# First experts of a four-layer model kernel: weights held and rows moving, third pieces of two blocks in the two halves of the array, no transposes between the products, weights loaded per block

## The chip, the core and the metric

The kernel runs on one core of a Trainium2 chip. The metric is the device time of one execution in microseconds (us). Times of single instructions are in nanoseconds (ns) where the view gives them so.

## The reference, cut to what matters

The model has four layers on x of shape (8, 512, 256), all in f32: linear attention, a mixture of 8 experts (two for each token) with a shared expert, windowed attention, and a mixture of 8 experts (one for each token). The change lies in the second layer:

```python
hg = jnp.einsum('th,ehi->eti', xf, wg)        # xf: 4096 tokens x 256; wg, wu: 8 x 256 x 352
hu = jnp.einsum('th,ehi->eti', xf, wu)
eo = jnp.einsum('eti,eih->eth', jax.nn.silu(hg) * hu, wd)     # wd: 8 x 352 x 256
y = jnp.einsum('te,eth->th', wdense, eo)      # wdense: two weights a token, else 0
shared = jax.nn.silu(xf @ swg) * (xf @ swu) @ swd
return (y + shared).reshape(B, S, H)
```

## The kernel before, in words

A stage that is called mix here does the first attention, the shared expert and the routing. Routing sorts the 8192 (token, expert) pairs into 71 blocks (`NBLK0`) of 128 rows, each block with one expert, whose number is in `blk_expert`. Then `pe_experts0` and its counterparts on the other engines run the first experts, block by block. Then come the windowed attention and the second experts.

For block b of the first experts:

- GpSimd (POOL) gathers the 128 rows from `normed` in HBM into one of three buffers `xs0` (L1839, `pool_rows`).
- TensorE (PE) transposes them, two transposes of 128x128 (L715, `pe_turn_rows`); ScalarE (ACT) copies the result to `xsT0` (L1076).
- PE computes the up products (L757). The transposed rows are the operand that is held in the array, 128x128, and the expert's weights move past it, 352 columns at a time: `wg` into one PSUM bank, `wu` into another. The weights of all eight experts, 5.8 MB, lie in SBUF as `wu0`; four loads of 1408 KB put them there at the kernel's start (L2027).
- ACT takes the silu of the first bank into `hsil` (L1085), VectorE (DVE) multiplies by the second (L1647). The result has tokens on the partitions.
- PE transposes it in three pieces of 128, 128 and 96 (L745), DVE copies them to `aT0` (L1641, L1642).
- PE computes the down product (L736): `aT0` held in three pieces, `wd0` moving, 256 columns. DVE copies it to `y0` (L1634), and SyncE (SP) stores it to `results` (L2044).

Each f32 matmul of the program is two instructions in the trace, each with its own load of the held operand (LDWEIGHTS, engine PEld), so L757 has 8 a block, L736 6; a transpose is one.

No scheduler is involved: each engine's order is that of the Python loops. In step s of `pe_experts0`, PE does the down product of block s-5, the transposes of the product of block s-4, the up products of block s-3 and the transposes of the rows of block s-2. A wait on a semaphore stops everything behind it on that engine. The waits in the PE code are the bank's last reader (`fill`), and the semaphore of the operand. SP's own queue in this stage holds the 71 stores of results and nothing else; SP issues a DMA in the order of its program, and waits at a wait. The register that picks an expert's weights (`value_load` of `blk_expert`) is read on PE, twice a block.

Of the kernel before, what the change touches and what calls it, by code (L numbers as in the profile page):

```python
# [44 lines left out]
DC = 3  # L45
IC = [P, P, INTER - 2 * P]
SC = [P] * 5 + [SI - 5 * P]
NC = len(SC)
# [139 lines left out]
def build(nc, a, out):  # L188
    ctx = ExitStack()
    with ctx:  # L190
# [3 lines left out]
        def sem(name):  # L194
            return ctx.enter_context(nc.semaphore(name))
# [66 lines left out]
        wu0 = carve(arena, 0, NX, EC, 2 * INTER)  # L262
        wd0 = carve(arena, 11264, NX, DC, E)
# [62 lines left out]
        y0 = carve(work, 5376, 3, E)  # L326
        hsil = carve(work, 6144, 2, INTER)
        aT0 = carve(work, 6848, 2, DC * P)

# [16 lines left out]
        x_loaded = [sem(f"x_loaded{b}") for b in range(B)]  # L346
        wa_loaded, bias_loaded, wu0_loaded, wd0_loaded, sh_loaded, wc_loaded = (
            sem(n) for n in ("wa_loaded", "bias_loaded", "wu0_loaded", "wd0_loaded", "sh_loaded", "wc_loaded"))
        w1_got, w2_got = ([sem(f"{n}_got{i}") for i in range(2)] for n in ("w1", "w2"))
# [16 lines left out]
        xsT_made, y_made = ([sem(f"{n}_l{l}") for l in range(2)] for n in ("xsT_made", "y_made"))  # L366
        sil0_made, hsil_made, aT0_made, h_made, tokens_made, part_made = (
            sem(n) for n in ("sil0_made", "hsil_made", "aT0_made", "h_made", "tokens_made", "part_made"))
        (picked, counted, so_far_made, placed, pick_step, scored, experts_listed, list_set, one_hot_made,
# [20 lines left out]
        def emptied(kind, *k):  # L390
# [34 lines left out]
            if kind == "up0":  # L425
                b, u = k
                return (sil0_made, hsil_made)[u], b + 1
            if kind == "h0":
                return aT0_made, k[0] + 1
            if kind == "down0":  # L430
# [289 lines left out]
        def pe_experts0(e):  # L720
            o_ring = (6, 7)
            e.wait_ge(route_step, EXPERT_AT)
            e.wait_ge(wu0_loaded, 16 * 4)
            e.wait_ge(wd0_loaded, 16 * 3)
            for s in range(NBLK0 + 5):
                b = s - 5
                if b == NBLK0 - 1:

                    pe_shared_up(e, BM, 0, FIRST_RING, range(1))
                if b >= 0:  # L730
                    bk = next_of(o_ring)
                    fill(e, ("down0", b), bk)
                    e.wait_ge(aT0_made, b + 1)
                    x = e.value_load(blk_expert[0:1, 0, b:b + 1], min_val=0, max_val=NX - 1)
                    for c in range(DC):
                        m = e.matmul(psum[:, bk, 0:E], aT0[0:IC[c], b % 2, c * P:(c + 1) * P],  # L736
                                     wd0[0:IC[c], bass.ds(x, 1), c, :], start=(c == 0), stop=(c == DC - 1))
                    m.then_inc(bank_full[bk], 1)
                b = s - 4
                if 0 <= b < NBLK0:  # L740
                    bk = next_of(T_RING)
                    fill(e, ("h0", b), bk)
                    e.wait_ge(hsil_made, b + 1)
                    for c in range(DC):
                        m = e.transpose(psum[0:IC[c], bk, c * P:(c + 1) * P], hsil[:, b % 2, c * P:c * P + IC[c]],  # L745
                                        ident[:, :])
                    m.then_inc(bank_full[bk], 1)
                b = s - 3
                if 0 <= b < NBLK0:
                    pair = ((2, 3), (0, 1))[b % 2]  # L750
                    e.wait_ge(xsT_made[0], b + 1)
                    for u in range(2):
                        fill(e, ("up0", b, u), pair[u])
                    x = e.value_load(blk_expert[0:1, 0, b:b + 1], min_val=0, max_val=NX - 1)
                    for u in range(2):
                        for c in range(EC):
                            m = e.matmul(psum[:, pair[u], 0:INTER], xsT0[:, b % 2, c * P:(c + 1) * P],  # L757
                                         wu0[:, bass.ds(x, 1), c, u * INTER:(u + 1) * INTER],
                                         start=(c == 0), stop=(c == EC - 1))
                        m.then_inc(bank_full[pair[u]], 1)  # L760
                b = s - 2
                if 0 < b < NBLK0:
                    pe_turn_rows(e, 0, b, xs0, next_of(T_RING))

# [307 lines left out]
        def act_turned_rows(e, l, b, xsT):  # L1072
            if b >= 2:
                e.wait_ge(*done["up0" if l == 0 else "up1", b - 2, 1])
            e.wait_ge(*done["rows", l, b])
            e.activation(xsT[:, b % 2, :], psum[:, bank_of["rows", l, b], 0:E], ACT.Copy).then_inc(xsT_made[l], 1)  # L1076

        def act_experts0(e):
            for s in range(NBLK0 + 5):
                b = s - 3  # L1080
                if 0 <= b < NBLK0:
                    if b >= 2:
                        e.wait_ge(*done["h0", b - 2])
                    e.wait_ge(*done["up0", b, 0])
                    e.activation(hsil[:, b % 2, :], psum[:, bank_of["up0", b, 0], 0:INTER],  # L1085
                                 ACT.Silu).then_inc(sil0_made, 1)
                b = s - 2
                if 0 <= b < NBLK0:
                    act_turned_rows(e, 0, b, xsT0)

        def act_attention(e):
# [535 lines left out]
        def dve_experts0(e):  # L1627
            for s in range(NBLK0 + 5):
                b = s - 5
# [5 lines left out]
                b = s - 4  # L1635
                if 0 <= b < NBLK0:
                    bk = bank_of["h0", b]
                    if b >= 2:
                        e.wait_ge(*done["down0", b - 2])
                    e.wait_ge(*done["h0", b])  # L1640
                    e.tensor_copy(aT0[:, b % 2, 0:2 * P], psum[:, bk, 0:2 * P])  # L1641
                    e.tensor_copy(aT0[0:IC[2], b % 2, 2 * P:3 * P], psum[0:IC[2], bk, 2 * P:3 * P]).then_inc(aT0_made, 1)  # L1642
                b = s - 3
                if 0 <= b < NBLK0:
                    e.wait_ge(sil0_made, b + 1)
                    e.wait_ge(*done["up0", b, 1])
                    e.tensor_tensor(hsil[:, b % 2, :], hsil[:, b % 2, :], psum[:, bank_of["up0", b, 1], 0:INTER],  # L1647
                                    ALU.mult).then_inc(hsil_made, 1)

# [356 lines left out]
        def sp_second_weights(e, k):  # L2006
            if k < 2:
                e.wait_ge(*done["again", (NU - 4, NU - 2)[k], TPB - 1, G - 1])
            else:
# [3 lines left out]
                        a["w2"][bass.ds(x, 1), :, :].rearrange("x p n -> p (x n)")).then_inc(w2_got[k % 2], 16)  # L2013

        def sp_mix(e):
            for b in range(B):
# [7 lines left out]
            e.dma_start(sdn[0:SC[5], 5, :], a["swd"][5 * P:SI, :]).then_inc(sh_loaded, 16)  # L2024
            for i, n in enumerate(("wg", "wu")):
                for c in range(EC):
                    e.dma_start(wu0[:, :, c, i * INTER:(i + 1) * INTER],  # L2027
                                a[n][:, c * P:(c + 1) * P, :].rearrange("x p n -> p x n")).then_inc(wu0_loaded, 16)
            for c in range(DC):
# [10 lines left out]
        def _(e):  # L2040
            sp_mix(e)
            for b in range(NBLK0):
                e.wait_ge(y_made[0], b + 1)
                e.dma_start(results[b * P:(b + 1) * P, :], y0[:, b % 3, :]).then_inc(result_kept[b % 3], 16)  # L2044
# [51 lines left out]
```

## Time and profile before

| what | value |
|---|---|
| three runs | 1450.71, 1465.5, 1467.46 us; median 1465.5 |
| profiled execution, span | 1452.0 us |
| first experts in it | about 308 to 617 us |
| PE busy, share of the span | 1394.5 us, 96% |
| DVE, ACT, POOL busy | 699.3, 467.8, 446.9 us |
| DMA over the span | 204.29 MB, mean 141 GB/s |

The profile also cuts the span in 40 slices of 36.3 us. In those of the first experts PE is 9 tenths busy or more, the DMA engines 1 to 2 tenths, at 50 to 70 GB/s. In the second experts, from about 1145 us on, which load their weights for each block, the DMA engines are 9 tenths busy at 320 to 350 GB/s. The granted clock of TensorE is 1.0 of full speed (2.4 GHz) in most slices.

Busy time counts from a matmul's start to its modelled end, and successive matmuls overlap; so what a matmul costs in a row of them is the distance between two starts, not its mean duration. In a merged row of the timeline, with n instructions in a time t and one of them taking d, that distance is (t - d)/(n - 1).

### The profile page before, as it was taken

The page shows a single profiled execution, that of the slowest core. Times are in us where ns is not written, and L with a number is a line of the kernel's source. Part 1 is how long each engine was busy: PE and PEld are TensorE (multiplying, and loading weights), DVE is VectorE, ACT ScalarE, POOL GpSimd, SP SyncE. Part 2 cuts the span into 40 slices and gives each one's busy share as a digit, 9 for nine tenths or more (in the row PEclk, how much of TensorE's full clock was granted, in tenths as well). Part 3 has the DMA queues.
Part 4 walks back from the last instruction along what each step waited for, and adds up shares of the span by engine and source line. Part 5 has one row for each costly group of instructions (what it writes and reads, how often), then busy time and mean ns, then how long its engine had stood idle before and what let it go on. Part 6 is the DMA issues. An engine that isn't in the chain of part 4 may idle for free.

```text
span 1452.0 us, 23966 instructions
## 1 busy us (share of the span) xinstructions
PE 1394.5 (96%) x7789; PEld 1034.4 (71%) x7789; DVE 699.3 (48%) x2502; ACT 467.8 (32%) x915; POOL 446.9 (31%) x533
## 2 busy tenths in 40 slices
PE   6899999999999999999999999999998999999998
PEld 4666655667777777755666667666666789999998
DVE  5743345723333333334878878788778213210000
ACT  1211111012111111121576665666656512111111
POOL 1100000035222222161444544544423434344442
PEclk9889999999999999999999999999999999999999
DMA  9400100011121211114544635545432578899996
GB/s 333 140 15 30 58 1 0 1 37 62 60 65 58 66 59 61 50 54 116 166 133 135 186 113 153 161 137 142 140 115 68 191 295 330 330 321 346 337 345 217
DMA packets 88583, 204.29 MB, mean 141 GB/s; under 512 B 11373, under 2 KB 45295, under 8 KB 78480
## 3 DMA queue, kind: packets, MB, share of 16 engines
q1 hardware_dynamic: 72512, 167.99, 35.4%
q0 software_dynamic: 12096, 32.13, 7.3%
q10 hardware_dynamic: 3856, 2.64, 0.6%
q8 instruction: 67, 1.10, 0.3%
q14 instruction: 52, 0.43, 0.1%
HBM read 151.48 MB, written 52.17 MB: 140 GB/s over the span
## 4 chain that ended last, share of the span: by engine, by line
PE 86%; DVE 7%; issue 4%; ACT 2%; DMA 0%; DVEq 0%; POOLq 0%; POOL 0%; ACTq 0%
PE psum L757 12%; PE psum L633 10%; PE psum L924 10%; PE psum L934 9%; PE psum L736 6%; PE psum L644 6%; PE psum L830 5%; PE psum L783 5%; PE psum L854 3%; PE psum L805 3%; DVE work L1763 2%; PE psum L884 2%; PE psum L560 2%; PE psum L863 2%; PE psum L715 2%
## 5 line engine op out<-in xcount | busy, mean ns | idle before, releaser
L1763 DVE CUSTOM_DVE_ANT_0 work<-psum,mask 128x384 bf16<-128x384 f32 (+1 forms) x512 | 230.8, 485 | 71.7 <-PE psum L783 69.3
L757 PE MATMUL psum<-arena,work 128*128 x568 | 185.0, 469 | 0.6 <-issue 0.6
L783 PE MATMUL psum<-kz,qT 96*128 96x384 f32 (+1 forms) x512 | 171.0, 401 | 13.5 <-DVE small L1763 12.6
L1839 POOL DMA_INDIRECT work<-normed,token_of x71 | 67.3, 948 | 342.3 <-PE psum L715 206.6
L633 PE MATMUL psum<-arena 128*128 128x512 f32 x320 | 152.3, 621 | 0.0
L924 PEld LDWEIGHTS psum<-arena 128*128 128x128 f32 x1248 | 145.3, 192 | 2.2 <-issue 0.4
L924 PE MATMUL psum<-arena 128*128 128x128 f32 x1248 | 146.1, 275 | 0.0
L1158 ACT ACTIVATE arena<-psum 128x384 f32<-128x384 f32 x256 | 112.2, 494 | 91.7 <-PE psum L805 90.8
L934 PE MATMUL psum<-arena 128*128 128x256 f32 x624 | 141.0, 379 | 0.0
L757 PEld LDWEIGHTS psum<-arena,work 128*128 128x128 f32 x568 | 102.1, 189 | 51.4 <-issue 2.3
L783 PEld LDWEIGHTS psum<-kz,qT 96*128 96x128 f32 x512 | 89.8, 194 | 66.5 <-DVE small L1763 40.3
L1624 DVE TENSOR_TENSOR arena<-psum,arena 128x256 f32<-128x256 f32 x39 | 16.6, 425 | 245.1 <-PE psum L934 245.1
L805 PE MATMUL psum<-qT,kz 100*128 100x384 f32 (+1 forms) x512 | 128.9, 328 | 3.8 <-ACT arena L1158 3.6
L934 PEld LDWEIGHTS psum<-arena 128*128 128x128 f32 x624 | 115.6, 190 | 14.1
L1905 POOL TENSOR_SCALAR_AFFINE_SELECT arena<-arena 128x512 f32<-128x512 f32 x96 | 63.0, 656 | 179.1 <-ACT arena L1158 161.5
L1186 ACT ACTIVATE arena<-psum 128x1024 f32<-128x1024 f32 x39 | 39.9, 1023 | 223.8 <-PE psum L924 223.8
L633 PEld LDWEIGHTS psum<-arena 128*128 128x128 f32 x320 | 62.4, 200 | 67.9 <-issue 66.7
L736 PE MATMUL psum<-arena,work 128*128 (+1 forms) x426 | 104.0, 380 | 0.2 <-issue 0.2
L805 PEld LDWEIGHTS psum<-qT,kz 100*128 100x128 f32 x512 | 89.7, 193 | 14.7 <-ACT arena L1158 12.9
L1647 DVE TENSOR_TENSOR work<-work,psum 128x352 f32<-128x352 f32 x71 | 37.0, 521 | 130.7 <-PE psum L757 130.7
L1160 ACT ACTIVATE arena<-psum 128x512 f32<-128x512 f32 x128 | 75.7, 596 | 57.6 <-PE psum L805 57.1
L644 PE MATMUL psum<-arena,work 128*128 128x256 f32 (+1 forms) x384 | 91.7, 381 | 2.3 <-DVE X L1324 2.3
(226 smaller groups left out, 2070.7 us busy)
## 6 DMA issues: line engine op xcount, KB each, us to landing
arena<-in_w SPq DMA_DIRECT2D x78, 1024.0 KB, 7.1
strips<-hi SPq DMA_DIRECT2D x64, 256.0 KB
kz<-strips SPq DMA_DIRECT2D x64, 192.0 KB, 3.1
qT<-strips SPq DMA_DIRECT2D x32, 384.0 KB, 4.6
results<-work SPq DMA_DIRECT2D x71, 128.0 KB, 1.7
strips<-lo SPq DMA_DIRECT2D x32, 256.0 KB
normed<-work SPq DMA_DIRECT2D x14, 512.0 KB, 3.0
X<-in_x SPq DMA_DIRECT2D x8, 512.0 KB, 9.5
```

The costliest lines, as they stand in the source:

```text
L633: m = e.matmul(psum[0:w, bk, :], sgu[:, k, u, c * P:c * P + w], xnT_all[:, b, k, :], start=(k == 0), stop=(k == EC - 1))
L644: m = e.matmul(psum[:, banks[t // 2], (t % 2) * E:(t % 2 + 1) * E], aT_s[0:w, q, t * P:(t + 1) * P], sdn[0:w, c, :], start=(c == 0 and t % ...
L736: m = e.matmul(psum[:, bk, 0:E], aT0[0:IC[c], b % 2, c * P:(c + 1) * P], wd0[0:IC[c], bass.ds(x, 1), c, :], start=(c == 0), stop=(c == DC ...
L757: m = e.matmul(psum[:, pair[u], 0:INTER], xsT0[:, b % 2, c * P:(c + 1) * P], wu0[:, bass.ds(x, 1), c, u * INTER:(u + 1) * INTER], start=(c ...
L783: m = e.matmul(psum[:, bk, at:at + w], qT[0:ROWS_S, slot, half, i * P:(i + 1) * P], kz[slot][0:ROWS_S, hd, lo_key:hi_key], start=True, sto ...
L805: m = e.matmul(psum[:, bk, at:at + w], kz[slot][0:ROWS_T, hd, j * P:(j + 1) * P], qT[0:ROWS_T, slot, half, lo_q:hi_q], start=True, stop=True)
L830: m = e.matmul(psum[32 * hh:32 * hh + 32, bk, lo:hi], v32[:, b % 2, j, G * g + hh, :], pT(u, j)[:, hh, 0:hi - lo], start=(j == 0), stop=(j ...
L924: m = e.matmul(psum[:, bk, q * P:(q + 1) * P], w1_now[k % 2][:, c, at:at + P], xsT1[:, k % 2, c * P:(c + 1) * P], start=(c == 0), stop=(c ...
L934: m = e.matmul(psum[:, bk, 0:E], hT1[:, k % 2, c * P:(c + 1) * P], w2_now[k % 2][:, c, :], start=(c == 0), stop=(c == HC - 1))
L1158: e.activation(pT(u, j)[:, hd, 0:w], psum[:, bk, 0:w], ACT.Exp, scale=1.0 / E ** 0.5).then_inc(p_exped, 1)
L1160: e.activation(pT(u, j)[:, hd - 1:hd + 1, 0:w], psum[:, bk, :].rearrange("p (h n) -> p h n", h=2), ACT.Exp, scale=1.0 / E ** 0.5).then_inc ...
L1763: e.tensor_tensor_reduce(masked[:, n % 2, 0:w], psum[:, bank_of["scores", u, i, hd], at:at + w], mask[:, P - off:P - off + w], 1.0, MASKED ...
```

## The change

The up products change sides. `pe_up0` holds 128x128 pieces of the weights in the array and moves the 128 transposed rows past them; the product comes out with the intermediate features on the partitions, as the down product needs it. The transposes of L745 and DVE's copies L1641 and L1642 are gone. Features 0 to 255 of `wg` and `wu` are four pieces (two of each), all in one PSUM bank. The last 96 features of each are split in 64 and 32: the 64 of both make one held piece of 128 columns; the 32 of both make one of 64 columns, and those of an even block go to the lower 64 columns of the array, those of the odd block after it to the upper 64. These third pieces are computed for two blocks at a time, in `pe_rest0`, after the odd block's `pe_up0`.

`wu0` now has four buffers of one block's weights each (5632 bytes in each partition, 704 KB). SP loads them per block from `wgu`, an array made on the host before the launch with `wg` and `wu` side by side in the order of use. The down product, the gathers and the transposes of the rows stay; `aT0` has four buffers instead of two. On PE the order within step s is now up (s-3), the third pieces if s-3 is odd, rows (s-2), down (s-5).

```diff
-            e.wait_ge(wu0_loaded, 16 * 4)
             e.wait_ge(wd0_loaded, 16 * 3)
             for s in range(NBLK0 + 5):
+                b = s - 3
+                if 0 <= b < NBLK0:
+                    pe_up0(e, b)
+                    if ends_pair(b):
+                        pe_rest0(e, pair_of(b))
+                b = s - 2
+                if 0 < b < NBLK0:
+                    pe_turn_rows(e, 0, b, xs0, next_of(T_RING))
                 b = s - 5
...
+        def pe_up0(e, b):
+
+            e.wait_ge(xsT_made[0], b + 1)
+            e.wait_ge(wu0_got[b % 4], 16 * (b // 4 + 1))
+            fill(e, ("up0", b), b % 2)
+            for q in range(4):
+                for c in range(EC):
+                    m = e.matmul(psum[:, b % 2, q * P:(q + 1) * P], wu0[:, b % 4, c, q * P:(q + 1) * P],
+                                 xsT0[:, b % 2, c * P:(c + 1) * P], start=(c == 0), stop=(c == EC - 1))
+            m.then_inc(bank_full[b % 2], 1)
+
+        def pe_rest0(e, pair):
+
+            q, bk = pair[0] // 2, 2 + pair[0] // 2 % 2
+            fill(e, ("rest0", q), bk)
+            for b in pair:
+                for c in range(EC):
+                    m = e.matmul(psum[:, bk, b % 2 * P:(b % 2 + 1) * P], wu0[:, b % 4, c, 4 * P:5 * P],
+                                 xsT0[:, b % 2, c * P:(c + 1) * P], start=(c == 0), stop=(c == EC - 1))
+            for c in range(EC):
+                for b in pair:
+                    half = b % 2 * D0
+                    m = e.matmul(psum[half:half + 2 * TAILS[1], bk, 2 * P:3 * P], wu0[:, b % 4, c, 5 * P:2 * INTER],
+                                 xsT0[:, b % 2, c * P:(c + 1) * P], start=(c == 0), stop=(c == EC - 1),
+                                 skip_group_check=True)
+            m.then_inc(bank_full[bk], 1)
...
             for s in range(NBLK0 + 5):
+                b = s - 3
+                if 0 <= b < NBLK0:
+                    if b >= 4:
+                        e.wait_ge(*done["down0", b - 4])
+                    e.wait_ge(sil0_made, b + 1)
+                    e.tensor_tensor(aT0[:, b % 4, 0:2 * P], sil0[:, b % 2, :],
+                                    psum[:, bank_of["up0", b], 2 * P:4 * P], ALU.mult).then_inc(main_made, 1)
+                    if ends_pair(b):
+                        dve_rest0(e, pair_of(b))
                 b = s - 5
...
+        def sp_up0_weights(e, b):
+
+            if b >= 4:
+                e.wait_ge(*done["rest0", (b - 4) // 2])
+            x = e.value_load(blk_expert[0:1, 0, b:b + 1], min_val=0, max_val=NX - 1)
+            e.dma_start(wu0[:, b % 4, :, :].rearrange("p c n -> p (c n)"),
+                        a["wgu"][bass.ds(x, 1), :, :].rearrange("x p n -> p (x n)")).then_inc(wu0_got[b % 4], 16)
...
             sp_mix(e)
+            e.wait_ge(route_step, EXPERT_AT)
+            for b in range(4):
+                sp_up0_weights(e, b)
             for b in range(NBLK0):
+                if 4 <= b + 3 < NBLK0:
+                    sp_up0_weights(e, b + 3)
                 e.wait_ge(y_made[0], b + 1)
                 e.dma_start(results[b * P:(b + 1) * P, :], y0[:, b % 3, :]).then_inc(result_kept[b % 3], 16)
```

On ACT the silu of a block is now 256 columns, and after an odd block three more follow (`act_rest0`: one of 64x256, two of 32x128), ahead of the copy of the next rows to `xsT0`. On DVE `dve_rest0` is one product of 64x256 and two of 32x128.

PE's rows in the first experts, in the middle of the stage. Before, one step (L715 rows of a block, L734 the register and L736 the down product, L745 the transposes of the product, L757 the up products):

```order
L715 MATMUL psum<-ident,work 128x128 [waits rows_got1,xsT_made_l0]
L715 MATMUL psum<-ident,work 128x128
L734 TENSOR_LOAD blk_expert [waits aT0_made,y_made_l0]
L734 ISA x2
...
L736 MATMUL psum<-arena,work 128x256
L745 MATMUL psum<-ident,work 128x128 [waits hsil_made,aT0_made]
L745 MATMUL psum<-ident,work 128x128
L745 MATMUL psum<-ident,work 96x128
L754 TENSOR_LOAD blk_expert [waits hsil_made,sil0_made,xsT_made_l0]
```

Now, the step of an odd block and the head of the next (L763 the four pieces, L773 the 64-feature pieces of two blocks, L778 the 32-feature pieces, L718 the rows, L746 the down product):

```order
L763 MATMUL psum<-work,arena 128x128 [waits main_made,wu0_got3,xsT_made_l0]
L763 MATMUL psum<-work,arena 128x128 x7
L773 MATMUL psum<-work,arena 128x128 [waits aT0_made]
L773 MATMUL psum<-work,arena 128x128 x3
L778 MATMUL psum<-work,arena 64x128 x4
L718 MATMUL psum<-ident,work 128x128 [waits rows_got0,xsT_made_l0]
L718 MATMUL psum<-ident,work 128x128
...
L746 MATMUL psum<-arena,work 128x256
L763 MATMUL psum<-work,arena 128x128 [waits main_made,wu0_got0,xsT_made_l0]
L763 MATMUL psum<-work,arena 128x128 x7
```

The up products moved ahead of the down product of their step, and their first matmul waits for a weight load's semaphore `wu0_got`.

SP's rows. Before, around and in this stage (the loads at the kernel's start are L2027, the stores L2044):

```order
L2027 DMA arena<-in_wg 128x8x352 x2
L2027 DMA arena<-in_wu 128x8x352 x2
...
L2036 DMA arena<-in_wqkvT 128x2x768 [waits bank_full6,bank_full7]
L2037 DMA arena<-in_wpT 128x2x256
L2044 DMA results<-work 128x256 [waits y_made_l0] x71
```

Now, in the middle of the stage (L2091 the store, L2057 and L2058 the load of weights):

```order
L2091 DMA results<-work 128x256 [waits y_made_l0]
L2057 TENSOR_LOAD blk_expert [waits bank_full3]
L2057 ISA x2
L2058 ISA
L2058 DMA arena<-in_wgu 128x1408
L2091 DMA results<-work 128x256 [waits y_made_l0]
```

The load of block b+3's weights stands behind the store of block b-1's result, and so behind the wait for it.

DVE's rows now, two steps in the middle of the stage (L1666 the product of the four pieces, L1681 and L1685 those of the third pieces, L1675 the copy of the down product):

```order
L1666 TENSOR_TENSOR work<-work,psum 128x256 [waits sil0_made,bank_full7]
L1681 TENSOR_TENSOR work<-work,psum 64x2x128 [waits rest_sil]
L1685 TENSOR_TENSOR work<-work,psum 32x128 x2
L1675 COPY work<-psum 128x256 [waits bank_full7,result_kept0]
L1666 TENSOR_TENSOR work<-work,psum 128x256 [waits sil0_made,bank_full6]
L1675 COPY work<-psum 128x256 [waits bank_full6,result_kept1]
```

In the step of an odd block the copy of a down product now stands behind the three products of the third pieces.

## Rows read from the trace of the kernel before

**Rows 1.** Windows: busy us (count) by engine, granted clock, DMA share, GB/s.

```profile
308.00:617.00 309.00, 307.74 (x1352) 222.41 (x1351) 105.63 (x285) 59.70 (x141) 80.25 (x79) 1.00 0.19 60
```

**Rows 2.** Timeline, middle of the stage: start, us, engine, line, count [idle before].

```profile
441.46 0.49 PE L745 MATMUL psum<-ident,work 128*128 128x128 f32 x3
441.73 0.42 DVE L1634 COPY work<-psum 128x256 f32<-128x256 f32 x1 [0.99 <-PE psum L736]
...
441.80 2.59 PE L757 MATMUL psum<-arena,work 128*128 x8
...
442.19 0.32 SPq L2044 DMA_DIRECT2D results<-work  x1
...
444.22 0.38 PE L715 MATMUL psum<-ident,work 128*128 128x128 f32 x2
...
444.44 1.46 PE L736 MATMUL psum<-arena,work 128*128 x6
...
445.74 0.49 PE L745 MATMUL psum<-ident,work 128*128 128x128 f32 x3
```

**Rows 3.** Timeline and group, second experts: 128 columns moving past 128 held.

```profile
1254.33 3.73 PE L924 MATMUL psum<-arena 128*128 128x128 f32 x32
...
L924 PE MATMUL psum<-arena 128*128 128x128 f32 x1248 | 146.1, 275 | 0.0
```

**Rows 4.** Timeline and group: 32 held columns; 128 held columns at 512 moving.

```profile
1140.12 2.36 PE L830 MATMUL psum<-arena 128*32 128x256 f32 x32
...
617.33 4.88 PE L633 MATMUL psum<-arena 128*128 128x512 f32 x11
...
L633 PE MATMUL psum<-arena 128*128 128x512 f32 x320 | 152.3, 621 | 0.0
```

**Rows 5.** Timeline, mix: from 128 held columns to 64.

```profile
118.86 2.02 PE L575 MATMUL psum<-arena,work 128*128 128x128 f32 x16
...
120.81 1.07 PE L581 MATMUL psum<-work,arena 128*64 128x512 f32 x2
```

**Rows 6.** Groups: ACT and DVE forms nearest the new ones; busy, mean ns.

```profile
L1076 ACT ACTIVATE work<-psum 128x256 f32<-128x256 f32 x71 | 27.2, 383 | 67.6 <-PE psum L715 67.6
L1642 DVE COPY work<-psum 96x128 f32<-96x128 f32 x71 | 19.7, 277 | 0.0
```

**Rows 7.** Lines L2002 and L2003 on SP: ns min/median/max, first and last start.

```profile
L2002 SPq TENSOR_LOAD <-blk_expert x39: 263/273/623, 1122.2 to 1426.3; - x39
L2003 SPq DMA_DIRECT2D arena<-in_w x39: 337/338/387, 1123.1 to 1427.1; - x39
```

**Rows 8.** DMA issues: KB each, us from issue to landing; 1123:1129, then the stage.

```profile
arena<-in_w SPq DMA_DIRECT2D x1, 1024.0 KB, 4.9
...
results<-work SPq DMA_DIRECT2D x70, 128.0 KB, 1.7
```

**Rows 9.** Timeline: four of PE's six idle times over 1.2 us at full clock.

```profile
47.73 2.02 PE L575 MATMUL psum<-arena,work 128*128 128x128 f32 x16 [2.10 <-DVE work L1234]
...
249.50 1.75 PE L644 MATMUL psum<-arena,work 128*128 128x256 f32 x7 [2.31 <-DVE X L1324]
...
689.63 0.92 PE L783 MATMUL psum<-kz,qT 96*128 96x384 f32 x2 [1.38 <-DVE small L1763]
...
1130.42 0.82 PE L805 MATMUL psum<-qT,kz 100*128 100x384 f32 x2 [1.29 <-ACT arena L1158]
```

**Rows 10.** Windows as rows 1, of the stretches behind these four.

```profile
49.70:56.50 6.80, 5.37 (x31) 3.54 (x31) 5.98 (x21) 1.19 (x2) 2.66 (x2) 1.00 0.25 83
249.50:256.30 6.80, 6.80 (x28) 4.51 (x29) 3.12 (x7) 0.60 (x1) 0.00 (x0) 1.00 0.01 2
692.20:699.00 6.80, 5.86 (x22) 4.85 (x21) 4.39 (x23) 1.57 (x3) 1.12 (x2) 0.50 0.45 138
1132.50:1139.30 6.80, 6.80 (x30) 6.44 (x29) 2.09 (x9) 1.64 (x4) 1.20 (x2) 0.50 0.00 0
```

**Rows 11.** Timeline: 512-column matmuls at half the clock.

```profile
150.92 5.91 PE L633 MATMUL psum<-arena 128*128 128x512 f32 x7
```

More of the change, by code:

```diff
@@ L46 @@
 IC = [P, P, INTER - 2 * P]
+TAILS = (D0, INTER - 2 * P - D0)
 SC = [P] * 5 + [SI - 5 * P]
@@ L259, in carve @@
             return v
-        wu0 = carve(arena, 0, NX, EC, 2 * INTER)
+        wu0 = carve(arena, 0, 4, EC, 2 * INTER)
         wd0 = carve(arena, 11264, NX, DC, E)
@@ L326, in build @@
         y0 = carve(work, 5376, 3, E)
-        hsil = carve(work, 6144, 2, INTER)
-        aT0 = carve(work, 6848, 2, DC * P)
+        sil_thin = carve(work, 4864, P)
+        sil_wide = carve(work, 4992, 2, P)
+        sil0 = carve(work, 6144, 2, 2 * P)
+        aT0 = carve(work, 6656, 4, DC * P)
         masked = carve(work, 4096, 2 * 3 * P // 2).bitcast(BF16).rearrange("p (s n) -> p s n", s=2)
@@ L346, in build @@
         x_loaded = [sem(f"x_loaded{b}") for b in range(B)]
-        wa_loaded, bias_loaded, wu0_loaded, wd0_loaded, sh_loaded, wc_loaded = (
-            sem(n) for n in ("wa_loaded", "bias_loaded", "wu0_loaded", "wd0_loaded", "sh_loaded", "wc_loaded"))
+        wa_loaded, bias_loaded, wd0_loaded, sh_loaded, wc_loaded = (
+            sem(n) for n in ("wa_loaded", "bias_loaded", "wd0_loaded", "sh_loaded", "wc_loaded"))
+        wu0_got = [sem(f"wu0_got{i}") for i in range(4)]
         w1_got, w2_got = ([sem(f"{n}_got{i}") for i in range(2)] for n in ("w1", "w2"))
@@ L366, in build @@
         xsT_made, y_made = ([sem(f"{n}_l{l}") for l in range(2)] for n in ("xsT_made", "y_made"))
-        sil0_made, hsil_made, aT0_made, h_made, tokens_made, part_made = (
-            sem(n) for n in ("sil0_made", "hsil_made", "aT0_made", "h_made", "tokens_made", "part_made"))
+        sil0_made, main_made, rest_sil, aT0_made, h_made, tokens_made, part_made = (
+            sem(n) for n in ("sil0_made", "main_made", "rest_sil", "aT0_made", "h_made", "tokens_made", "part_made"))
         (picked, counted, so_far_made, placed, pick_step, scored, experts_listed, list_set, one_hot_made,
@@ L425, in emptied @@
             if kind == "up0":
[L426 to L429, printed above, removed]
+                return main_made, k[0] + 1
+            if kind == "rest0":
+                return aT0_made, min(2 * k[0] + 2, NBLK0)
             if kind == "down0":
@@ L735, in pe_experts0 @@
                     for c in range(DC):
-                        m = e.matmul(psum[:, bk, 0:E], aT0[0:IC[c], b % 2, c * P:(c + 1) * P],
+                        m = e.matmul(psum[:, bk, 0:E], aT0[0:IC[c], b % 4, c * P:(c + 1) * P],
                                      wd0[0:IC[c], bass.ds(x, 1), c, :], start=(c == 0), stop=(c == DC - 1))
                     m.then_inc(bank_full[bk], 1)
[L739 to L760, printed above, removed]
@@ L761, in pe_experts0, with pair_of, ends_pair @@
-                b = s - 2
-                if 0 < b < NBLK0:
-                    pe_turn_rows(e, 0, b, xs0, next_of(T_RING))
+        def pair_of(b):
+            return range(b - b % 2, b + 1)
+        def ends_pair(b):
+            return b % 2 == 1 or b == NBLK0 - 1
+        def pe_up0(e, b):
[7 more added lines that the diff above has]
+            m.then_inc(bank_full[b % 2], 1)
@@ L1073, in act_turned_rows @@
             if b >= 2:
-                e.wait_ge(*done["up0" if l == 0 else "up1", b - 2, 1])
+                e.wait_ge(*done["rest0", (b - 2) // 2] if l == 0 else done["up1", b - 2, 1])
             e.wait_ge(*done["rows", l, b])
@@ L1082, in act_experts0 @@
                     if b >= 2:
-                        e.wait_ge(*done["h0", b - 2])
-                    e.wait_ge(*done["up0", b, 0])
-                    e.activation(hsil[:, b % 2, :], psum[:, bank_of["up0", b, 0], 0:INTER],
+                        e.wait_ge(main_made, b - 1)
+                    e.wait_ge(*done["up0", b])
+                    e.activation(sil0[:, b % 2, :], psum[:, bank_of["up0", b], 0:2 * P],
                                  ACT.Silu).then_inc(sil0_made, 1)
+                    if ends_pair(b):
+                        act_rest0(e, pair_of(b))
                 b = s - 2
@@ L1089, in act_experts0, with act_rest0 @@
                     act_turned_rows(e, 0, b, xsT0)
+        def act_rest0(e, pair):
+            q, n, w = pair[0] // 2, len(pair), TAILS[1]
+            if q >= 1:
+                e.wait_ge(aT0_made, 2 * q)
+            e.wait_ge(*done["rest0", q])
+            bk = bank_of["rest0", q]
+            e.activation(sil_wide[0:D0, 0:n, :], psum[D0:2 * D0, bk, 0:n * P].rearrange("p (b n) -> p b n", b=n), ACT.Silu)
+            for b in pair:
+                half = b % 2 * D0
+                m = e.activation(sil_thin[half:half + w, :], psum[half + w:half + 2 * w, bk, 2 * P:3 * P], ACT.Silu)
+            m.then_inc(rest_sil, 1)
         def act_attention(e):
@@ L1628, in dve_experts0 @@
             for s in range(NBLK0 + 5):
+                b = s - 3
[5 more added lines that the diff above has]
+                                    psum[:, bank_of["up0", b], 2 * P:4 * P], ALU.mult).then_inc(main_made, 1)
+                    if ends_pair(b):
+                        dve_rest0(e, pair_of(b))
                 b = s - 5
@@ L1634, in dve_experts0, with dve_rest0 @@
                     e.tensor_copy(y0[:, b % 3, :], psum[:, bank_of["down0", b], 0:E]).then_inc(y_made[0], 1)
[L1635 to L1648, printed above, removed]
+        def dve_rest0(e, pair):
+            q, n, w = pair[0] // 2, len(pair), TAILS[1]
+            bk, s0 = bank_of["rest0", q], pair[0] % 4
+            e.wait_ge(rest_sil, q + 1)
+            e.tensor_tensor(aT0[0:D0, s0:s0 + n, 2 * P:3 * P], sil_wide[0:D0, 0:n, :],
+                            psum[0:D0, bk, 0:n * P].rearrange("p (b n) -> p b n", b=n), ALU.mult)
+            for b in pair:
+                half = b % 2 * D0
+                e.tensor_tensor(aT0[D0:D0 + w, b % 4, 2 * P:3 * P], sil_thin[half:half + w, :],
+                                psum[half:half + w, bk, 2 * P:3 * P], ALU.mult).then_inc(aT0_made, 1)
         def dve_attention(e):
@@ L2024, in sp_mix @@
             e.dma_start(sdn[0:SC[5], 5, :], a["swd"][5 * P:SI, :]).then_inc(sh_loaded, 16)
[L2025 to L2028, printed above, removed]
             for c in range(DC):
@@ L2080 @@
         "gate0T": g["L0_ffn_gate_w"].T,
-        "wg": g["L0_ffn_wg"], "wu": g["L0_ffn_wu"], "wd": g["L0_ffn_wd"],
+        "wgu": np.concatenate([g[n][:, :, i:j] for i, j, names in (
+            (0, 2 * P, ("L0_ffn_wg", "L0_ffn_wu")), (2 * P, 2 * P + D0, ("L0_ffn_wu", "L0_ffn_wg")),
+            (2 * P + D0, INTER, ("L0_ffn_wu", "L0_ffn_wg"))) for n in names], axis=2)
+               .reshape(NX, EC, P, 2 * INTER).transpose(0, 2, 1, 3).reshape(NX, P, EC * 2 * INTER),
+        "wd": g["L0_ffn_wd"],
         "swg": g["L0_ffn_swg"], "swu": g["L0_ffn_swu"], "swd": g["L0_ffn_swd"],
```

## The prediction

> **What bounds the kernel now.** I read the page first: PE is busy 96% of the span. So the question is whether the stage that changes is paced by PE. The windows view of that stage says yes: PE is busy 307.7 of 309 us, the granted clock is 1.00, DVE is busy a third of the time, and the DMA engines 0.19 of it [rows 1]. Then I read one step in the timeline. L745 starts at 441.46 and again at 445.74, so a block takes 4.28 us. It splits, by the distances between starts, into 0.34 us of L745, 2.42 of L757, 0.22 of L715 and 1.30 of L736 (six instructions, 0.217 each) [rows 2]. No row of PE in it shows idle time: the stage is PE's sum, 71 times. Nothing else is worth time here as long as it hides; and whatever makes PE wait costs in full.
>
> **PE's work after the change.** What L757 did is now done by matmuls that move only 128 columns. The nearest row is L924, the same form: 32 of them in 3.73 us, one lasting 0.275, so (3.73 - 0.275)/31 = 0.111 us each [rows 3]. The weight load of each hides at that pace. For a pair of blocks:
>
> - the four pieces: 2 x 16 instructions x 0.111 = 3.55 us;
> - the 64-feature pieces: 8 x 0.111 = 0.89;
> - the 32-feature pieces: 8 instructions in two halves of the array. L830 holds 32 columns, four heads side by side; 32 of its instructions, half of 256 and half of 384 moving columns, take 2.36 us. At the pace of L633, (4.88 - 0.62)/10 = 0.43 us for 512 columns, they would take 8.5 us one by one, so four do run together [rows 4]. I take two together here: 4 x 0.111 = 0.45; one by one it is 0.89;
> - going to the half-width form and back: the first L581 starts 0.21 us after the last L575 (118.86 + 2.02 - 0.275 = 120.60), against 0.11 inside a row [rows 3, 5]. Above these 0.10 I take 0.15 for each change, since the weight load of the other form doesn't hide either: 0.30 a pair;
> - rows and down product stay: 2 x 0.22 + 2 x 1.30 = 3.04.
>
> The sum is 8.23 us a pair, against 8.56 now: 0.3 us less, 11 us over 35.5 pairs. If the halves don't overlap it is 5 us more than now instead. The removed DVE copies and the second register read on PE are worth nothing, since they lie beside PE's work. The 5.6 MB of loads at the start that fall away are worth nothing either: nothing in the stage before waits for them.
>
> **The added wait.** An odd step's PE work is 1.78 + 0.89 + 0.45 + 0.30 + 0.22 + 1.30 = 4.94 us, an even step's 1.78 + 0.22 + 1.30 = 3.30. The weights of block b+3 are asked for by SP after it has stored the result of block b-1, although their buffer came free a step or two earlier. That result is the last thing of step b+4; the weights are wanted by the first matmul of step b+6. One step lies between. For an odd block b+3 that step is an even one, 3.30 us. Against it stands this chain, from the end of the down product:
>
> - DVE starts 0.11 us later (L736 ends at 445.90, a block earlier at 441.62; L1634 starts at 441.73) and takes 0.42; SP issues the store 0.04 later, in 0.32 [rows 2];
> - in an odd step DVE first has the third pieces. After their last matmul ACT needs 0.1 + 0.38 + 2 x 0.28, DVE 0.06 + 0.42 + 2 x 0.28, by the nearest forms [rows 2, 6]: 2.1 us, while the down product is done 1.8 us after that matmul: 0.3 more;
> - SP then reads the register and issues the load: from the start of TENSOR_LOAD to the DMA, 0.8 us by first and last starts [rows 7];
> - the landing. 1024 KB alone take 4.9 us from the issue, 128 KB 1.7 [rows 8]; on the line between them 704 KB take 3.8. A gather and a store of 128 KB use the same engines in each step, for which I add 0.2: 4.0. The ends are 3.6 (no slower than the line, somewhat faster issue) and 4.9 (as the 1024 KB);
> - 0.1 to PE.
>
> Together 0.11 + 0.3 + 0.42 + 0.04 + 0.32 + 0.8 + 4.0 + 0.1 = 6.1 us. The next step could have started 0.16 before the down product's end (0.38 less 0.22). So PE stands idle 6.1 + 0.16 - 3.30 = 3.0 us before each odd block from about the fifth on: 33 times, 99 us. The ends of the landing make it 2.6 to 3.9, 86 to 129 us. Even blocks don't wait: between their chain's ends lie an odd step and that idle time, 7.9 us. Behind the waiting matmul stands everything of the step: third pieces, rows, down product; ACT, DVE, the gathers and the next load wait with it, so nothing catches up.
>
> **The clock.** An idle time of 3 us is longer than any that PE had at the full clock in this kernel after its start. Of six over 1.2 us I show four: 2.10 and 2.31 us went by and the clock stayed; 1.38 and 1.29, in stretches with other short gaps, were followed within 4 us by 6.8 us at 0.50, which is 1.2 instead of 2.4 GHz [rows 9, 10]. Of the two not shown one was followed by a fall. At 0.50 a matmul takes twice as long: seven L633 in 5.91 us, (5.91 - 0.62)/6 = 0.88 against 0.43 [rows 4, 11]. Each fall thus costs 3.4 us of work if it does not lie over another wait. I take a fall after 7 in 10 of the 33 waits, more than the half seen because these waits are longer: 23 x 3.4 = 78 us. The ends are 16 falls (54 us) and 33 (112 us).
>
> The Trainium skill (TensorE: Matmul & The Clock Gate, HAM oscillation) tells of a kernel that waits some microseconds for a DMA between bursts of matmuls and starts every burst at the lower clock. It speaks against this change. By it all 33 waits are followed by a fall, and the sum below would be 34 us higher; the 2.10 and 2.31 us of these rows, shorter than its waits, had none.
>
> **The sum**, against the profiled execution's own span: 1452.0 - 11 + 99 + 78 = 1618 us. That execution lies 13.5 us below the median of the three runs and 1.3 above the fastest, and I don't know which the runs of the changed kernel will be like; I add half, 7: 1625 us.
>
> **The rivals.**
>
> - *The weights arrive in time.* Four buffers and loads issued three blocks ahead look like enough. Then only PE's work counts: 1452 - 11 + 7 = 1448 us, 1% faster. For it speaks that a load needs only 704 KB in 4.2 us, 170 GB/s, and the second experts move over 320. Against it speaks that this is a matter of when the load is issued: the break-even is an idle time of 0.33 us, a chain of 3.5 instead of 6.1 us, and the load would have to land in 1.4 us, less than 128 KB take now [rows 8].
> - *PE waits, but the clock holds.* 1452 - 11 + 99 + 7 = 1547 us. For it speak the two longest idle times of the trace, after which it held [rows 9, 10]; and PE would be busy 8.2 of 11.2 us.
> - *The clock falls after every wait.* PE waits for a landing of 704 KB, works 8.2 us, waits again, and each of the 33 waits is followed by 6.8 us at 0.50: 1452 - 11 + 99 + 112 + 7 = 1659 us. For it speaks that 1.3 us were enough twice. The Trainium skill's page above has this rule.
> - *Everything at its dear end.* The load takes 4.9 us to land and the halves of the array work one after the other: 30 and 16 us on the forecast, 1671 us. For it speaks that gathers and stores share the engines.
>
> **How the numbers follow.** The forecast, that PE waits and the clock falls after most waits, has a chance of 0.50; its own range is 1588 to 1666 (landing and falls at their ends). The clock holds: 0.18. It falls every time: 0.17. The dear end: 0.07. In time: 0.08. The range 1530 to 1670 leaves out the case in time, part of the dear end and the tails of the others, some 0.2 in all. A measurement of this kernel can tell about 2% from no change. All cases but one are slower by more than that: 0.90; in time is within 2% of 1465.5: 0.08; that leaves 0.02 for faster, a clock in step with cheaper third pieces.
>
> **What would show it.** In the stage of the first experts: L763's first matmul of odd blocks idle about 3 us before it, with the DMA arena<-in_wgu as the releaser, and none before even ones; a pair of blocks at 8.2 us of PE work where the clock is 1.00; the load's landing near 4 us; L778's instructions starting two by two; windows at 0.50 for 6 or 7 us, some 23 of them. The stage would be about 475 us long instead of 309. The prediction is wrong if the waits are short or absent, which would mean that SP gets to the load earlier than the chain says, and off in size if the clock's falls are few or many.

## The result

| | median of runs | runs | span of the profiled execution |
|---|---|---|---|
| before | 1459.99 us | 1450.71, 1454.49, 1465.5, 1467.46 | 1452.0 |
| changed | 1596.83 us | 1588.97, 1593.91, 1599.75, 1600.77 | 1592.0 |

The changed kernel takes 1.094 times as long, 95% interval 1.089 to 1.098. The page of its profile, the parts that changed:

```profile
PE 1431.0 (90%) x8712; PEld 1117.1 (70%) x8712; DVE 690.0 (43%) x2467; ACT 491.6 (31%) x1022; POOL 447.9 (28%) x533
...
L763 PE MATMUL psum<-work,arena 128*128 128x128 f32 x1136 | 169.4, 311 | 101.9 <-issue 98.8
...
arena<-in_wgu SPq DMA_DIRECT2D x71, 704.0 KB, 4.4
```

L763, the four pieces, has 101.9 us of idle time of PE before it, 97.9 of them before the 33 odd blocks from block 5 on and the rest before blocks 0, 1, 2 and 4; L757 of before had none to speak of, and its stage was busy throughout [rows 1]. The releaser is given as "issue", that is, the profile doesn't name what was waited for. The windows of the stage, as rows 1 for before:

```profile
301.30:748.00 446.70, 346.34 (x2275) 305.07 (x2276) 94.43 (x248) 83.05 (x248) 80.45 (x79) 0.90 0.46 149
```

The stage of the first experts is 446.7 us long, from its first up product to the end of its last down product; in the kernel before it was 309.2. That is 137.5 us more. The spans of the two profiled executions differ by 140.0 and the medians by 136.8, so nearly all of the loss is here. The mean granted clock of the stage is 0.90 where it was 1.00. The timeline of a pair of blocks, which answers to rows 2:

```profile
446.78 0.38 PE L746 MATMUL psum<-arena,work 96*128 x1
447.00 0.59 DVE L1685 TENSOR_TENSOR work<-work,psum 32x128 f32<-32x128 f32 x2
447.00 2.05 PE L763 MATMUL psum<-work,arena 128*128 128x128 f32 x16
447.63 0.42 DVE L1675 COPY work<-psum 128x256 f32<-128x256 f32 x1
448.08 0.33 SPq L2091 DMA_DIRECT2D results<-work  x1
448.89 0.38 PE L718 MATMUL psum<-ident,work 128*128 128x128 f32 x2
449.11 1.46 PE L746 MATMUL psum<-arena,work 128*128 x6
...
449.49 0.35 SPq L2058 DMA_DIRECT2D arena<-in_wgu  x1
...
451.13 0.33 SPq L2091 DMA_DIRECT2D results<-work  x1
452.22 0.34 SPq L2058 DMA_DIRECT2D arena<-in_wgu  x1
453.56 0.77 PE L763 MATMUL psum<-work,arena 128*128 128x128 f32 x4 [2.98 <-issue]
```

The down product of an odd step ends at 447.16. DVE copies its result only at 447.63, since it had the third pieces to do (L1685 just ahead). SP stores it at 448.08 and issues the load at 449.49. PE has done the even step by 450.57 and stands idle until 453.56, 4.07 us after the issue. Past block 4 the idle time comes before odd blocks only. In the median of the 33 odd blocks it is 2.01 us from the end of that down product to the load's issue, and 4.27 from there to the first matmul. The clock, in windows around that place:

```profile
454.00:457.40 3.40, 3.40 (x19) 3.40 (x18) 0.00 (x0) 0.38 (x1) 0.00 (x0) 0.50 0.41 171
433.50:454.00 20.50, 14.65 (x108) 12.54 (x107) 4.92 (x13) 4.31 (x13) 3.79 (x4) 1.00 0.52 165
```

Right behind the idle time the clock is at 0.50 for 3.4 us, and PE then does 19 matmuls where at the full clock it does 30. The trace's record of the clock has 24 such stretches in the stage, 85.3 us in all: 23 of 3.4 us and one of 6.8. Each begins during the wait before an odd block or at most 1.4 us after it. For 1.7 of the 85.3 us PE stood idle anyway, so they cost (85.3 - 1.7)/2 = 41.8 us of work. The pairs of blocks show the same: from block 11 on the median is 11.37 us for a pair without such a stretch and 13.12 for a pair with one, 1.75 more.

### The profile page after: what moved, and what is told of

It is laid out like the page before. It is cut to its first block, busy times and chain, and to the rows that moved or that the text cites. A ratio compares the mean times of both kernels' runs of the same rounds, so it can differ in the third digit from the quotient of the medians.

```text
span 1592.0 us, 25699 instructions
## 1 busy us (share of the span) xinstructions
PE 1431.0 (90%) x8712; PEld 1117.1 (70%) x8712; DVE 690.0 (43%) x2467; ACT 491.6 (31%) x1022; POOL 447.9 (28%) x533
## 4 chain that ended last, share of the span: by engine, by line
PE 81%; issue 10%; DVE 6%; ACT 2%; POOL 1%; DMA 1%; DVEq 0%; POOLq 0%; ACTq 0%
PE psum L763 10%; PE psum L942 9%; PE psum L952 9%; PE psum L636 8%; PE psum L746 6%; PE psum L647 5%; PE psum L801 5%; PE psum L848 5%; PE psum L823 3%; PE psum L872 3%; PE psum L773 3%; PE psum L902 2%; PE psum L718 2%; PE psum L563 2%; PE psum L881 2%
## 5 line engine op out<-in xcount | busy, mean ns | idle before, releaser
L763 PE MATMUL psum<-work,arena 128*128 128x128 f32 x1136 | 169.4, 311 | 101.9 <-issue 98.8
L763 PEld LDWEIGHTS psum<-work,arena 128*128 128x128 f32 x1136 | 154.7, 218 | 123.6 <-issue 112.1
L636 PE MATMUL psum<-arena 128*128 128x512 f32 x320 | 146.1, 599 | 0.0
L1666 DVE TENSOR_TENSOR work<-work,psum 128x256 f32<-128x256 f32 x71 | 29.9, 421 | 255.3 <-ACT work L1103 253.4
L1103 ACT ACTIVATE work<-psum 128x256 f32<-128x256 f32 x71 | 27.3, 384 | 305.7 <-PE psum L763 305.7
L746 PE MATMUL psum<-arena,work 128*128 (+1 forms) x426 | 103.8, 380 | 0.0
```

The source lines that it names most:

```text
L636: m = e.matmul(psum[0:w, bk, :], sgu[:, k, u, c * P:c * P + w], xnT_all[:, b, k, :], start=(k == 0), stop=(k == EC - 1))
L746: m = e.matmul(psum[:, bk, 0:E], aT0[0:IC[c], b % 4, c * P:(c + 1) * P], wd0[0:IC[c], bass.ds(x, 1), c, :], start=(c == 0), stop=(c == DC ...
L763: m = e.matmul(psum[:, b % 2, q * P:(q + 1) * P], wu0[:, b % 4, c, q * P:(q + 1) * P], xsT0[:, b % 2, c * P:(c + 1) * P], start=(c == 0), ...
```

## Experiments

All are edits of the changed kernel. "Stage" is measured as above, "idle" is PE's idle time before L763 by its row, "falls" are the stretches at 0.50 that begin in the stage and their length in all. In the runs marked * one stretch of 3.4 us lies at the head of the stage, behind 1.5 us of idle time before block 0; it has nothing to do with the loads. Five rows are single executions: the two that load less, the one that loads nothing, and the two with one half of the array. The three that load less or nothing leave wrong weights in the buffers, and are here for their traces.

| kernel | time | stage | idle | falls |
|---|---|---|---|---|
| before | 1460 | 309.2 | - | 0 |
| changed | 1597 | 446.7 | 101.9 | 24, 85.3 us |
| DVE copies the result first * | 1571 | 421.3 | 76.2 | 17, 58.0 |
| half of each load * | 1527 | 376.6 | 63.5 | 5, 17.1 |
| an eighth of each load * | 1486 | 333.5 | 26.7 | 1, 3.4 |
| wait filled with work * | 1560 | 407.2 | 15.1 | 1, 3.4 |
| loads one block earlier * | 1451 | 304.2 | 3.4 | 0, the one at the head begins 0.06 us ahead of it |
| no loads * | 1451 | 302.3 | 3.2 | 1, 3.4 |
| earlier loads, one half of the array, blocks in turn * | 1484 | 317.5 | 3.1 | 1, 3.4 |
| earlier loads, one half of the array, block by block * | 1470 | 317.7 | 3.3 | 1, 3.4 |
| earlier loads, ACT copies the rows first | 1452 | 305.6 | 5.8 | 0 |

**Loads one block earlier.**

```diff
-                if 4 <= b + 3 < NBLK0:
-                    sp_up0_weights(e, b + 3)
+                if b + 4 < NBLK0:
+                    sp_up0_weights(e, b + 4)
```

> The only edit: SP issues the load of block b+4's weights where it issued that of block b+3, so each load has one more step of PE work to hide behind (8.2 us between the store it stands behind and the use, against a chain of 6.1). Theory (the loss is the place of the load in SP's order, and the clock's falls follow from the wait): no wait of PE for arena<-in_wgu, no fall of the clock in the stage, a stage of about 310 us (PE work 8.2 us a pair, and 0.3 us a pair in which PE waits for ACT's copy of the rows), and a time within 1% of the kernel before, 1450 to 1470 us. Rival (the loads themselves cost: 51 MB share the DMA engines with gathers and stores, or the held-weights form is slower on PE than L924 says): the time stays over 1500 us.

Measured: 1451.2 us, 0.996 times the kernel before (0.992 to 0.9995), with all of the change's matmuls, loads and silus in it.

```profile
440.30 1.46 PE L746 MATMUL psum<-arena,work 128*128 x6
441.61 1.95 PE L763 MATMUL psum<-work,arena 128*128 128x128 f32 x16
443.39 1.06 PE L773 MATMUL psum<-work,arena 128*128 128x128 f32 x8
444.38 0.66 PE L778 MATMUL psum<-work,arena 128*64 128x128 f32 x8
444.96 0.44 PE L718 MATMUL psum<-ident,work 128*128 128x128 f32 x2
445.24 1.46 PE L746 MATMUL psum<-arena,work 128*128 x6
446.54 2.05 PE L763 MATMUL psum<-work,arena 128*128 128x128 f32 x16
448.43 0.38 PE L718 MATMUL psum<-ident,work 128*128 128x128 f32 x2
448.65 1.46 PE L746 MATMUL psum<-arena,work 128*128 x6
449.95 0.27 PE L763 MATMUL psum<-work,arena 128*128 128x128 f32 x1
```

This is its timeline of PE: a pair of blocks from 441.61 to 449.95, 8.34 us without idle time. No odd block waits. One fall lies at the head of the stage, where none was expected. Everything lost was lost by the place of the load in SP's order; traffic and form of the product cost nothing against the kernel before. The theory stands, and its rival falls.

**No loads.** The load in SP's loop is taken out and the wait for it, from block 4 on.

> Loads only the weights of the first four blocks and none after them, and PE doesn't wait for more, so most blocks use the wrong experts' weights. It shows what PE's own order costs with no load and no wait. Theory: a stage of 305 to 312 us at a clock of 1.00, as in the run with the loads one block earlier, and the same time as that one within its noise. Rival (the loads' traffic slows gathers or stores even when nobody waits for the weights): this one is faster than that one by 10 us or more.

Measured: 1450.7 us, stage 302.3 against 304.2, a little under the expected 305. The traffic of 48 MB of weights, once nobody waits for it, costs at most 2 us.

**The wait filled with work.**

```diff
+            fill(e, ("up0", b), b % 2)
+            if b % 2 == 1 and b >= 5:
+                for _ in range(3):
+                    e.matmul(psum[:, b % 2, :], ident[:, :], wd0[:, 0, 0:2, :].rearrange("p c n -> p (c n)"),
+                             start=True, stop=True)
             e.wait_ge(wu0_got[b % 4], 16 * (b // 4 + 1))
-            fill(e, ("up0", b), b % 2)
```

> The changed kernel with work added: before the up products of each odd block from 5 on PE does three f32 matmuls of 512 columns (2.6 us at the full clock) into the bank that the up products then overwrite, ahead of the wait for the weights. It separates the wait's own length from the clock. Theory (each fall of the clock to 0.50 after a wait costs half its length, 34 falls of 3.4 us in the stage, 58 us): falls in the stage go to nearly none, and the time goes down by 45 to 60 us, to about 1540 us, although there is more work. Rival (the falls cost nothing, since the chain through SP sets the pace and PE's slower work hides in it): the time stays within 10 us of the changed kernel's, or goes up.

Measured: 1560.2 us, 37 us less than the changed kernel with 198 matmul instructions more; 1.072 times the kernel before (1.067 to 1.078). PE's timeline and the stage's window:

```profile
440.33 2.74 PE L762 MATMUL psum<-arena,ident 128*128 128x512 f32 x6
443.56 2.05 PE L767 MATMUL psum<-work,arena 128*128 128x128 f32 x16 [0.49 <-DMA arena<-in_wgu]
...
303.00:710.20 407.20, 393.74 (x2473) 305.25 (x2474) 94.43 (x248) 82.99 (x248) 80.26 (x79) 1.00 0.51 164
```

With 0.5 us of this wait left (0.24 in the median), the profile names what ended it, the load. The clock's mean is 1.00, and the stage is 39.5 us shorter. The 41.8 us of the 24 falls, less the one at the head of this stage, would be 40.1. So the falls cost what half their length says, on top of the wait; they don't hide in the chain. The rival falls. The time went down by less than the expected 45 to 60 us, since that expectation took 34 falls where there are 24.

**Less to load.** From block 4 on only the first 704, or 176, of a partition's 1408 numbers are brought.

> The changed kernel, but from block 4 on each load brings only the first half of a block's weights (352 KB), the other half being stale, so those blocks' results are wrong. SP's order is unchanged. Theory (PE's wait is the chain through SP less one even step): the landing goes from 4.4 to about 2.9 us and the idle time before odd blocks from 2.9 to about 1.4 us, 33 x 1.5 = 50 us less; the falls become fewer, so 1480 to 1545 us. Rival (the wait is set by something of fixed length, such as the register read or DVE's order, and not by the landing): the idle time stays over 2.5 us.

> As the run with half a load, but from block 4 on each load brings an eighth of a block's weights (88 KB), so those blocks' results are wrong. With the landing near that of a store of 128 KB, about 1.8 us instead of 4.4, the theory gives an idle time of 2.9 - 2.6 = 0.3 us before odd blocks, no fall of the clock in the stage, and a stage of 304 + 33 x 0.3 = 314 us; the time about 1465 us. It is also the fixed part of the rule that the first rival needed: even a tiny load only just arrives. Rival (a fixed length other than the landing): the idle time stays over 1 us.

Measured: landings of 4.4, 3.0 and 2.0 us (704, 352 and 88 KB), idle times before odd blocks with a median of 2.9, 1.7 and 0.6 us, stages of 447, 377 and 334 us. The half is within its expected range (1527 us), with 0.3 us more idle time than expected. The eighth has 0.6 us of idle time where I expected 0.3; 0.2 of that is its landing, which I took at 1.8 us and which was 2.0. It is 20 us dearer than expected with a stage 20 us longer. The idle time of its 33 odd blocks is 13 us more than the 10 expected. Another 5 us are 0.16 lost at each wait, which I had left out: where PE waits, the last matmul before it runs to its end, and without a wait the next one starts 0.16 us earlier. Its stage has no fall behind a wait for a load, and that of the half has four. The idle time follows the landing nearly one to one (2.4 us less landing, 2.3 us less idle time). Even 88 KB come too late: of the chain of over 6 us, 2.0 are in front of the load.

**DVE's order.** In `dve_experts0` the copy of the down product's result goes ahead of `dve_rest0`.

> The changed kernel, with DVE's copy of the down product's result ahead of its three products of the third pieces; SP's order is that of the change. Theory (the load hangs on that copy through SP): the copy starts 0.1 us after the down product's end instead of 0.47, every load of an odd block is issued 0.36 us earlier, the idle time before odd blocks goes from 2.87 to about 2.5 us, 33 x 0.36 = 12 us less, and a few falls of the clock fewer: 1575 to 1585 us. Rival (the idle time is set by when the load's buffer comes free or by the DMA engines): it stays at 2.9 us.

Measured: 1570.9 us, 1.075 times the kernel before (1.068 to 1.082), 4 us under the expected range. One pair, DVE, SP and PE:

```profile
444.07 1.46 PE L746 MATMUL psum<-arena,work 128*128 x6
...
445.64 0.42 DVE L1673 COPY work<-psum 128x256 f32<-128x256 f32 x1 [2.25 <-PE psum L746]
...
447.26 0.38 PE L718 MATMUL psum<-ident,work 128*128 128x128 f32 x2
...
447.79 1.56 PE L746 MATMUL psum<-arena,work 128*128 x6
...
451.64 3.19 PE L763 MATMUL psum<-work,arena 128*128 128x128 f32 x16 [2.30 <-issue]
```

The copy starts 0.11 us after the down product's end (445.53), as expected. The idle time before odd blocks is 2.2 us in the median, 0.7 less and not 0.36. The rows show where the rest went: the even step's down product now starts 0.53 us after L718 instead of 0.22. By its program it waits for its `aT0`, which the third pieces complete, and then reads a register; in these rows `aT0` comes 1.0 us later behind the odd step's down product than in the pair shown of the changed kernel. So 0.3 us of waiting moved into the step. Net of that the pair has 0.4 less, near the 0.36 that the copy gives. Stage: 25.4 us less, near the sum of 33 x 0.36 = 12 and of the 12.8 us that the fewer falls are worth. That split is rough: among pairs without a fall the medians are 11.37 and 11.18 us, only 0.19 apart.

**The halves of the array.** In the kernel with the loads one block earlier, the odd block's 32-feature piece goes to the lower 64 columns too.

> The kernel with the loads one block earlier, in which the 32-feature pieces of the odd block also go to the lower 64 columns of the array (into other columns of the same PSUM bank), so that nothing of them runs side by side. Theory (the two halves work together, four groups of two at 0.10 to 0.11 us): their 8 instructions take 0.4 us more a pair, the stage is 14 to 16 us longer than the 304 us of the run with the halves. Rival (the starts that the trace shows 7 ns apart are only two queued instructions, and the array takes them one by one): no difference over 3 us.

> As the run with both 32-feature pieces in the lower half, in which those pieces were summed over two columns of weights in turn within the same partitions of one bank (its sums for them are not the reference's); here all of one block's piece comes before the other's. Theory (the halves work side by side in the change, and one by one in both of these): L778 to the rows' transposes again takes about 1.02 us instead of 0.59, and the stage is 13 to 15 us longer than 304 us. Rival (the extra time of that run came from the interleaved sums): 0.6 to 0.8 us.

Measured: L778 to L718 takes 1.02 us in the median of both, instead of 0.59, and the stages are 317.5 and 317.7 us instead of 304.2, 13 to 14 us more. The times of the two, 1484.0 and 1470.3 us, differ outside the stage, where the first has 28 us more at 0.50. So the eight L778, which side by side take 0.59 us to the next row, take 1.02 one by one:

```profile
445.28 1.09 PE L777 MATMUL psum<-work,arena 128*64 128x128 f32 x8
446.30 0.44 PE L718 MATMUL psum<-ident,work 128*128 128x128 f32 x2
```

These are rows of the second of the two (L777 is there the line of L778). The array does work on both halves at once. That saves 0.43 us a pair, 15 us in all by the pairs and 13 to 14 by the stages.

**ACT's order.** In the kernel with the loads one block earlier, ACT copies the next rows before the three silus.

> The kernel with the loads one block earlier, with ACT's copy of the next rows moved ahead of its three silus of the third pieces. In that kernel the first up matmul after an odd step starts on time but the second comes 0.10 us late (0.21 instead of 0.11). Theory (that is the wait for ACT's copy): up to 0.1 us a pair, 3 us, less than can be told from no change in the time, though the stage should be 300 to 302 us instead of 304. Rival (the silus then come too late for DVE and the down product of the even step waits): the stage gets longer than 304 us.

Measured: 1451.8 us, 0.995 times the kernel before (0.991 to 0.999). The even step's four pieces take 1.78 us to the next row instead of 1.89, so ACT's copy was what the second matmul waited for. But the stage is 305.6 us where 300 to 302 was expected, with three idle times of about 1 us that the profile puts down to no wait; nothing is gained that can be told. What those three are stays open. The rival had a part in it: in the even step the down product now takes 1.36 us to the next row instead of 1.30, which gives back half of the 0.11.

## Why the prediction was right

The measured 1596.8 us lie in the range of 1530 to 1670, 28 us under the forecast of 1625, in the case that had the highest chance.

- **PE's work.** Predicted 8.23 us a pair, 11 us less over the stage. Measured, with no waits, 8.34 us a pair, and a stage 5.0 us shorter than before (304.2 against 309.2), in which the fall at its head costs 1.7. The terms: four pieces 1.78 us as predicted and 1.89 in an even step, where ACT's copy is 0.1 late; 64-feature pieces with the change of form 0.99, where 0.89 + 0.15 was predicted; the halves with the change back 0.59, where 0.45 + 0.15 was predicted; the rows behind them 0.28, where 0.22 was. L924 of rows 3 was the right row.
- **The wait.** Predicted 3.0 us lost before each of 33 odd blocks, 99 us, none before even ones. Measured 2.88 us of idle time in the median; 0.16 more is lost at each, since without a wait the next step starts that much before the last matmul's end, as the prediction's chain counts too. That is 97.9 + 5.3 = 103.2 us in all. The chain's pieces: 0.47 us to the copy (0.41 predicted), 0.76 from the store's end to the load's issue in the median (0.8; the 1.08 of the pair shown is an exception), 4.27 from issue to matmul (4.1), and 3.41 for the even step that hides part of it (3.30). The wait of block 5 was shorter, 1.85 us, and those of blocks 7 and 9 were longer, 4.3 and 4.7.
- **The clock.** Predicted 23 falls of 3.4 us of work, 78 us. There were 24, but all except one were 3.4 us long and not 6.8 as in rows 10, so together 41.8 us of work. This is the term that was mis-sized, and with it the forecast's distance: 36 us of it one way, and 6 of PE's work and 4 of the wait the other. That the count came out is in part luck: "7 in 10" was a judgment from three falls behind six waits. That falls follow from the wait and cost extra is shown by the filled wait and by the earlier loads.
- **The Trainium skill's rule** (TensorE: Matmul & The Clock Gate, HAM oscillation), that the engine is at the lower clock after every such wait, held after 24 of the 33 waits of odd blocks. Its direction was right, and as a count it was a bound.
- **The rivals.** In time: excluded by the idle times; even 88 KB don't come in time. The clock holds: excluded by the record of the clock. A fall after every wait: 24 of 33. The dear end: the landing was 4.4 us in the median of all loads, 4.2 in that of the odd blocks' and 4.0 in the pair shown, and the halves overlap.
- **The sum**, from the kernel with the loads one block earlier: 304.2, and 97.2 for idle time (PE stands idle 99.9 us within the changed stage and 2.7 within that one), 5.3 for the 0.16 us at each wait, and 40.1 for the clock (41.8 less 1.7) give 446.8 against 446.7 measured. The parts outside the stage took 1142.8 us before and 1145.3 after.
- **A slip in the range.** The prediction gives the forecast's own case an upper end of 1666 us. With the ends that it names, 30 us for the landing and 34 for the falls, that end is 1689.

## What to carry to other kernels

When a transfer is moved from the start of a kernel into a loop, its bandwidth says little: write down what stands ahead of it in the issuing queue, add the landing time, and compare that chain with the engine's work between there and the use. Here four buffers gave room for three blocks, but a load queued behind a store of the result left one short step of room; issuing it one block earlier, two lines, turned 1.094 into 0.996. And a wait that recurs on TensorE costs more than its length, as long as it lets the clock fall: filling it with useless matmuls gave back 37 us.

## What the hardware showed that I had not expected

The stretches at half clock behind these waits were 3.4 us long, 23 of 24, while those of rows 10, in other stages, were 6.8; why they differ is not shown. How often the clock fell went with the length of the idle time: behind 33 waits with medians of 2.9, 2.2, 1.7 and 0.6 us, recurring every 9 to 13 us, it fell 24, 16, 4 and 0 times. The four of the half load came behind waits of 1.96 to 2.70 us, among its longer ones. But the length does not decide it alone: in the changed kernel the waits with a fall had a median of 2.90 us and the nine without one 2.86. And SP's own path is not always the same: from a store's end to the issue of the next load, with a register read between, it took 0.76 us in the median and 0.8 at most in 64 of 67 steps, but 1.08, 1.09 and 1.64 in the other three.
